# A one-core transformer block: output tiles inside a batch's last attention unit, next tokens prepared a unit earlier, denominators ahead of values

## What is computed

```python
def _tc_rmsnorm(x, t, gw, gb, bw, bb):
    g = (t @ gw.T + gb)[:, None, :]
    b = (t @ bw.T + bb)[:, None, :]
    inv_rms = jax.lax.rsqrt(jnp.mean(x * x, axis=-1, keepdims=True) + EPS)
    return g * x * inv_rms + b

def _attention(x, Wq, Wk, Wv, Wo):          # 16 heads of 32
    q, k, v = ((x @ W.T).reshape(B, L, H, dh) for W in (Wq, Wk, Wv))
    attn = jnp.einsum('blhd,bmhd->bhlm', q, k) / scale
    p = jax.nn.softmax(attn, axis=-1)
    o = jnp.einsum('bhlm,bmhd->blhd', p, v).reshape(B, L, D)
    return o @ Wo.T

x1 = x + _attention(_tc_rmsnorm(x, t, g1w, g1b, b1w, b1b), Wq, Wk, Wv, Wo)
y = x1 + _swiglu(_tc_rmsnorm(x1, t, g2w, g2b, b2w, b2b), gate_w, hid_w, out_w)
out = x + y
```

## Time and profile before

| | |
|---|---|
| median of 3 runs | 2479.52 us (2472.38 to 2492.58) |
| the profiled execution | 2483.76 us, of which the span 2481.9 us |
| busy: PE | 2309.7 us (93%) |
| busy: PE weight loads | 1572.9 us (63%) |
| busy: DVE | 1676.2 us (68%) |
| busy: ACT | 1310.9 us (53%) |
| busy: POOL | 1454.4 us (59%) |
| mean granted TensorE clock | 0.976 of full speed |

### The profile page before, as it was taken

How to read it: one execution, slowest core, us unless ns; L and a number is a source line. 1 busy time by engine, 2 the same in 40 slices (tenths; PEclk the granted TensorE clock), 3 DMA queues, 4 the chain that set the end, 5 groups by cost and what they waited for, 6 DMA issues and landing times. The chain is left out here.

```text
span 2481.9 us, 40287 instructions
## 1 busy us (share of the span) xinstructions
PE 2309.7 (93%) x10884; PEld 1572.9 (63%) x10884; DVE 1676.2 (68%) x2732; ACT 1310.9 (53%) x2319; POOL 1454.4 (59%) x1351
## 2 busy tenths in 40 slices
PE   5999989999989999989999848999999999999999
PEld 4655436554447555456554336888888888888887
DVE  4776734667725776537777347887788778778877
ACT  3366762566752667734667724445444534454454
POOL 0388981689970888944889925731572166216711
PEclk8999999999989999999999978999999999999999
DMA  5212203212122122132222043115412541254125
GB/s 179 81 41 63 64 14 108 52 41 67 48 71 64 38 69 52 47 95 52 51 57 60 21 162 136 60 60 179 151 54 69 170 154 52 74 164 157 47 81 174
DMA packets 92656, 209.60 MB, mean 84 GB/s; under 512 B 15632, under 2 KB 15632, under 8 KB 90640
## 3 DMA queue, kind: packets, MB, share of 16 engines
q1 hardware_dynamic: 91344, 202.71, 27.2%
q0 software_dynamic: 1088, 4.19, 0.4%
HBM read 134.23 MB, written 19.92 MB: 62 GB/s over the span
## 5 line engine op out<-in xcount | busy, mean ns | idle before, releaser
L680 DVE TENSOR_REDUCE pmax<-bank 128x1 f32<-128x512 f32 x1024 | 653.7, 684 | 197.0 <-PE bank L893 187.6
L599 ACT ACTIVATE probs<-bank 128x512 f32<-128x512 f32 x1024 | 572.0, 600 | 330.6 <-PE bank L973 249.5
L447 POOL TENSOR_TENSOR sums<-sums,probs 128x512 f32<-128x512 f32 x512 | 641.4, 1291 | 0.5 <-ACT probs L599 0.5
L447 POOL TENSOR_TENSOR sums<-probs 128x512 f32<-128x512 f32 x256 | 320.4, 1282 | 380.6 <-ACT probs L599 258.9
L973 PE MATMUL bank<-qs,ks 128*128 128x512 f32 x1024 | 441.3, 439 | 40.0 <-ACT probs L599 37.9
L893 PE MATMUL bank<-ks,qs 96*128 96x512 f32 x1024 | 402.9, 406 | 25.8 <-DVE pmax L680 25.1
L973 PEld LDWEIGHTS bank<-qs,ks 128*128 128x128 f32 x1024 | 192.8, 191 | 323.4 <-ACT probs L599 167.3
L1536 PE MATMUL bank<-H_hi,wt_hi 128*128 128x512 f32 x896 | 350.0, 391 | 14.6 <-DVE H_lo L1391 14.6
L1550 PE MATMUL bank<-ow,aw 128*128 128x512 f32 x1536 | 358.7, 392 | 0.0
L1536 PE MATMUL bank<-H_lo,wt_hi 128*128 128x512 f32 x896 | 349.6, 390 | 0.0
L1536 PE MATMUL bank<-H_hi,wt_lo 128*128 128x512 f32 x896 | 349.5, 390 | 0.0
(11 more groups left out here) (139 smaller groups left out, 3233.8 us busy)
## 6 DMA issues: line engine op xcount, KB each, us to landing
raw<-in_gu_w SPq DMA_DIRECT2D x66, 512.0 KB, 3.6
wo_raw<-in_out_w SPq DMA_DIRECT2D x128, 256.0 KB, 2.6
ks<-qk_hi SPq DMA_DIRECT2D x136, 128.0 KB, 2.4
qs<-qk_hi SPq DMA_DIRECT2D x264, 64.0 KB, 2.0
x<-in_x SPq DMA_DIRECT2D x10, 1024.0 KB, 5.2
ks<-qk_lo SPq DMA_DIRECT2D x68, 128.0 KB, 2.4
qs<-qk_lo SPq DMA_DIRECT2D x132, 64.0 KB, 2.0
wv<-wv_parts SPq DMA_DIRECT2D x4, 2048.0 KB, 8.9
```

Source lines behind the costliest of these rows:

```text
L447: nc.gpsimd.tensor_tensor(sums[:, h, :], first, probs[:, s % 2, h, :], ALU.add) \
L599: nc.scalar.activation(probs[:, s % 2, h, :], sbank[i % SB][:], ACT.Exp, scale=SCALE).then_inc(st_done, 1)
L680: nc.vector.reduce_max(pmax[:, t, h, hf:hf + 1], mbank[n % MB][:], AX_X).then_inc(sq_done, 1)
```

## The change

- **Steps.** hT moves from units 5 and 7 to (unit, step) (4,15), (4,18), (4,24), (5,8) and (6,14), (6,17), (6,24), (7,0). What goes ahead of it moves too: `load_x` of the first half from SP's turn in unit 3 to unit 1, squares from (4,4) to (3,4) and from (6,3) to (5,5), the inverse roots on POOL from (4,5) to (3,6) and from (6,6) to (6,0), the scaling from (4,6) to (4,1) and from (6,7) to (6,2). The squares' unused output goes to a slot of `qk_hi` instead of `yout`. Projections of Q stand at every step, not every second one; the last K tile moves from step 26 of unit 7 to step 13.
- **Output tiles 0 and 1** stand in unit 7, two products a step, from steps 18 and 24. Their operand is split at (3,3) and (4,1), that of tile 2 at (7,1), and for these three ACT first copies the tokens to a free PSUM bank (`mspare`), from which both halves of the split are made.
- **Order.** Where a key tile has both, `denominators` stands ahead of `values`.
- **Sums.** Head 0 of quad 0 adds into a slot of `yout`, not `sums`, and POOL waits for the D product at its second add of a quad, not at the first.
- **Last key tile of a batch.** POOL doesn't add it (4 adds); TensorE multiplies `probs` by the ones directly (4 more products in that D product).
- **Normalising** the last two units' `o` moves from POOL to DVE; for unit 6 through a copy of `den` in `mspare` that ACT makes.
- **Tail.** D product, then tiles 2 to 7. SP waits for the D product before it loads `wv`.

```diff
@@ -32,17 +32,20 @@
 IN_V = {1: ("Q", 1), NT - 3: ("K", 2, 0), NT - 2: ("mT", 0)}
 UNIT = NS * GH
-PROJECTED = {("K", 2, 1): (0, 1), ("Q", 2): (9, 2)}
+PROJECTED = {("K", 2, 1): (0, 1), ("Q", 2): (9, 1)}
 for odd in (1, 3):
     PROJECTED.update({("Q", odd + 2): (odd * UNIT, 1), ("K", odd + 3, 0): (odd * UNIT + 14, 1),
-                      ("K", odd + 3, 1): ((odd + 1) * UNIT, 1), ("Q", odd + 3): ((odd + 1) * UNIT + 9, 2)})
-PROJECTED.update({("Q", NU - 1): (5 * UNIT, 1), ("Q", NU): (6 * UNIT + 8, 2), ("K", NU, 0): (7 * UNIT + 8, 1),
-                  ("K", NU, 1): (7 * UNIT + 26, 1)})
-HT_AT = {5: (9, 13, 17, 24), 7: (13, 16, 19, 23)}
+                      ("K", odd + 3, 1): ((odd + 1) * UNIT, 1), ("Q", odd + 3): ((odd + 1) * UNIT + 9, 1)})
+PROJECTED.update({("Q", NU - 1): (5 * UNIT, 1), ("Q", NU): (6 * UNIT + 8, 1), ("K", NU, 0): (7 * UNIT + 8, 1),
+                  ("K", NU, 1): (7 * UNIT + 13, 1)})
+HT_AT = {(4, 15): (0, 0), (4, 18): (1, 0), (4, 24): (2, 0), (5, 8): (3, 0),
+         (6, 14): (0, 1), (6, 17): (1, 1), (6, 24): (2, 1), (7, 0): (3, 1)}
 SUMS_AT = {(5, 1): (0, 0), (1, 1): (1, 1)}
 MAXIMA_AT = (6, 3)
+EARLY_OUT = {18: 0, 24: 1}
+SPLIT_AT = {(3, 3): 0, (4, 1): 1, (7, 1): 2}
 VALUES_AT = (3, 1, 3, 2)
 SB, MB = 3, 3
...
                         stack(b, ("Q", u + 2), (u + 2) % 3)
-                    if u == 3:
+                    if u == 1:
                         load_x(b, 0, prepared)
...
-                hold(sp, held, sum_done, sums_done(b, NU - 1, NS - 1, GH - 1))
+                hold(sp, held, w_ready, MISC(b, misc_index(True, ("D", NU - 1, 1)) + 1))
                 load_wv()
...
-                        if (u, s) == (4, 5):
+                        if (u, s) == (3, 6):
                             inverse_root(b, b * 2 + 2)
-                        if (u, s) == (6, 6):
+                        if (u, s) == (6, 0):
                             inverse_root(b, b * 2 + 3)
-                        if s == 4 and u:
+                        if s == 4 and 0 < u < NU - 1:
                             normalise(b, u - 1)
+                        if n == NU * NS - 1:
+                            pool.wait_ge(sum_done, sums_done(b, u, s - 1, GH - 1))
+                            pool.sem_inc(sum_done, GH)
+                            break
                         for h in range(GH if s % QT else 0):
                             pool.wait_ge(st_done, SCORES_T(b, NT + n * GH + h + 1) + SB)
-                            if s % QT == 1 and h == 0:
+                            if (u, s, h) == (0, 1, 0):
+                                pool.wait_ge(y_stored[0], b * (NT // 2 * 16) + 16)
+                            if s % QT == 1 and h == 1:
                                 pool.wait_ge(w_ready, MISC(b, sums_before(u, s // QT)))
                             if s % QT > 1:
                                 pool.wait_ge(sum_done, sums_done(b, u, s - 1, h))
-                            first = probs[:, 0, h, :] if s % QT == 1 else sums[:, h, :]
-                            nc.gpsimd.tensor_tensor(sums[:, h, :], first, probs[:, s % 2, h, :], ALU.add) \
+                            total = sum_place(s // QT, h)
+                            first = probs[:, 0, h, :] if s % QT == 1 else total
+                            nc.gpsimd.tensor_tensor(total, first, probs[:, s % 2, h, :], ALU.add) \
...
                     act.wait_ge(sq_ready, SCORES_Q(b, NU * NMAX + t - 1))
-                nc.scalar.activation(osplit[:, t % 2, 0, :, :], o[:, :, t * P:(t + 1) * P],
-                                     ACT.Copy).then_inc(os_act, 1)
+                tokens = o[:, :, t * P:(t + 1) * P]
+                if t in SPLIT_AT.values():
+                    up = mspare[:].rearrange("p (g c) -> p g c", g=NG)
+                    if t:
+                        act.wait_ge(os_dve, b * NT + t)
+                    nc.scalar.activation(up, tokens, ACT.Copy).then_inc(o_up, 1)
+                    act.wait_ge(o_up, b * len(SPLIT_AT) + (t + 1))
+                    tokens = up
+                nc.scalar.activation(osplit[:, t % 2, 0, :, :], tokens, ACT.Copy).then_inc(os_act, 1)
+            def denominators_up(b):
+                act.wait_ge(den_ready, b * (NU - 1) + (NU - 1))
+                act.wait_ge(sq_done, SCORES_Q(b, (NU - 1) * NMAX + NMAX) + MB)
+                nc.scalar.activation(mspare[:], den[:], ACT.Copy).then_inc(den_up, 1)
             def weight_hi(w):
...
-                            if (u, s) == (4, 4):
+                            if (u, s) == (3, 4):
                                 square(b, 0, h)
-                            if (u, s) == (4, 6):
...
                                 output(b, u - 1)
-                        if u == NU - 1 and s >= NS - 2:
-                            output_hi(b, s - (NS - 2))
+                            if u == NU - 1 and (s, h) == (2, 3):
+                                denominators_up(b)
+                            if u == NU - 1 and (s, h) in SPLIT_AT:
+                                output_hi(b, SPLIT_AT[s, h])
                 output(b, NU - 1)
-                for t in range(2, NT):
+                for t in range(len(SPLIT_AT), NT):
...
                     link(nc.vector.reciprocal(pair[:, 1, :], cols[:, :, 0]))
+                elif part == 2 and u == NU - 1:
+                    link(nc.vector.transpose(den[:], pair[:, 1, :].unsqueeze(2).to_broadcast([P, QB // 32, 32])))
+                elif part == 2:
+                    nc.vector.transpose(den[:], pair[:, 1, :].unsqueeze(2).to_broadcast([P, QB // 32, 32])).then_inc(den_ready, 1)
                 else:
-                    nc.vector.transpose(den[:], pair[:, 1, :].unsqueeze(2).to_broadcast([P, QB // 32, 32])).then_inc(den_ready, 1)
+                    dve.wait_ge(od_act, b * NU + (u + 2))
+                    if u < NU - 1:
+                        dve.wait_ge(den_up, b + 1)
+                    cols = o[:, u // 2, u % 2 * QB:(u % 2 + 1) * QB]
+                    nc.vector.tensor_tensor(cols, cols, den[:] if u == NU - 1 else mspare[:], ALU.mult).then_inc(on_done, 1)
...
+                def lo_part(t):
+                    dve.wait_ge(os_act, b * NT + t + 1)
+                    tokens = o[:, :, t * P:(t + 1) * P]
+                    if t in SPLIT_AT.values():
+                        tokens = mspare[:].rearrange("p (g c) -> p g c", g=NG)
+                    nc.vector.tensor_tensor(osplit[:, t % 2, 1, :, :], tokens,
+                                            osplit[:, t % 2, 0, :, :].bitcast(F32), ALU.subtract).then_inc(os_dve, 1)
...
                                     work_tile(b, tile)
-                            if s == 3 and u and h < 3:
+                            if s == 3 and 0 < u < NU - 1 and h < 3:
                                 normalise(b, u - 1, h)
-                def lo_part(t):
-                    dve.wait_ge(os_act, b * NT + t + 1)
-                    nc.vector.tensor_tensor(osplit[:, t % 2, 1, :, :], o[:, :, t * P:(t + 1) * P],
-                                            osplit[:, t % 2, 0, :, :].bitcast(F32), ALU.subtract).then_inc(os_dve, 1)
+                            if s == 2 and u == NU - 1 and h < 3:
+                                normalise(b, u - 1, h)
+                            if (u, s, h) == (NU - 1, 3, 0):
+                                normalise(b, u - 1, 3)
+                            if u == NU - 1 and (s, h) in SPLIT_AT:
+                                lo_part(SPLIT_AT[s, h])
                 def out_tile(t):
                     n = NU * NMAX + t
...
-                for t in range(2):
-                    lo_part(t)
                 out_tile(0)
-                for t in range(2, 4):
-                    lo_part(t)
+                lo_part(len(SPLIT_AT))
                 work_tile(b, ("D", NU - 1, 1))
-                for part in range(3):
+                for part in range(4):
                     normalise(b, NU - 1, part)
                 for t in range(1, NT):
...
-                pe.wait_ge(sum_done, sums_done(b, u, QT * quad + QT - 1, GH - 1))
+                direct = (u, quad) == (NU - 1, QUADS - 1)
+                pe.wait_ge(sum_done, sums_done(b, u, QT * quad + QT - 1 - direct, GH - 1))
                 for h in range(GH):
-                    last = nc.tensor.matmul(wbank[DH * h:DH * h + DH, :], ones[:], sums[:, h, :], start=True, stop=True)
+                    last = nc.tensor.matmul(wbank[DH * h:DH * h + DH, :], ones[:], sum_place(quad, h), start=True,
+                                            stop=not direct)
+                for h in range(GH if direct else 0):
+                    last = nc.tensor.matmul(wbank[DH * h:DH * h + DH, :], ones[:], probs[:, (NS - 1) % 2, h, :], start=False,
+                                            stop=True)
                 last.then_inc(w_ready, 1)
+            def out_tile(b, t, steps):
+                steps = [(k, a, c) for k in range(NG) for a, c in ((0, 0), (0, 1), (1, 0))][steps]
```

(26 more changed lines are left out.)

44 lines of the change are left out of this document (29 added, 15 removed).

## The result

The changed kernel takes **2466.69 us** (median of 15 runs, 2462.11 to 2472.02); beside it the kernel before took 2479.52 (15 runs, 2472.38 to 2492.58). The ratio is 0.9949, 95% interval 0.9938 to 0.9961: 13 us gained, not the 60 forecast, and the time lies outside the range. The profiled execution took 2466.27 us (span 2464.4, mean clock 0.975).

A forecast was written before the change was run, and what follows sets the result against it. TensorE, nearly full, was taken as the bound, POOL as second limit. Gains of 15.0 us a batch, 60 for four, plus 2.5 took the profiled 2483.8 to 2421.3; it said 2420, range 2400 to 2446.

The forecast's parts named there:

- is POOL's chain and hardly anything else: Unit 5 before, 31.83 us, taken as bounded by POOL's 31.3; 0.5 us a batch to be gained.
- last tail, beyond these: Batch 3's tail: stores and next loads start earlier, gaining 2.5 us more than the other tails' 5.0.
- D product first, POOL's wait later: Units 0, 1, 2, 5: POOL's first add runs beside the D product; gains 0.4, 1.2, 1.2, 0.5 us.
- Projections at every step only fill a step that was empty.: Attention's projections, at every step instead of every second: claimed to fill empty steps, with no cost charged.
- Unit 6: Earlier scaling, and inverse root inside the D product wait, leave about 33.2 us; gain 3.0, bounds 1 and 4.
- Unit 7: Fewer turns, two output tiles added, no last POOL adds: 31.7 us against 35.5, gain 3.8, bounds 2 and 5.
- the early tiles wait: Rival, unit 7: tile 0 or 1 stops TensorE 3 us each, 24 in all, 2444 us; chance 0.08.
- the clock stays low: Rival, unit 7: two units at clock 0.86 keep their 3.6 us over batch 3's, 2428 us; chance 0.05.
- Tail: Two output tiles leave, four products enter: 21 us against 26.4, gain 5.0; one store wait, 2 us taken.
- held by transfers: Rival, tail: store waits take 2 us from each of three tails, 7.5 from the last; 2433 us, chance 0.12.
- TensorE is full already: Rival: units 0 to 5 give nothing back; only unit 6, unit 7 and tail gain, 2436 us; chance 0.18.
- The D product blocks: Rival: 60 D products ahead of value products wait for POOL; at 2 us a place, 2537 us; chance 0.03.

The follow-up runs named there:

- the census: The kernel before with eight extra 128x4 tensor_scalar instructions a batch on DVE, in units 1, 2, 3 and 5: 2482.24 us, ratio 1.0004.

## Why the prediction was wrong

**The step that failed.** The prediction prices the loads, the squares, the inverse root and the turns, and has no term for the mean of squares, which moves with them from (4,5) to (3,5) and from (6,5) to (5,7) on DVE. It was put at nothing without being named. It cost 37.4 us: unit 5 came out 7.2 us longer where the prediction had it 0.5 shorter, and unit 3 gave back 0.2 us where it gives 1.9 without that instruction. The view that would have shown the danger was at hand: the group of this instruction in the kernel before has a mean of 1457 ns, for four numbers a partition. It takes nine times its own time there, each time to 0.03 us behind the end of a POOL instruction; so POOL's work beside it decides how long it lasts, and the change moved it to where the last eight of a row of adds were still to end. The prediction used the Trainium skill, SBUF — State Buffer, Who interferes with whom, only for the rest parts with two SBUF inputs, and gave its rule without its condition: an instruction with at most one SBUF input stays out of the contention only outside the modes that use both port pairs. The same section also names tensor_scalar among the VectorE instructions that can enter a mode which takes the port shared with GpSimd, and says that tensor_reduce never does on trn2. The runs agree with both: tensor_scalar 0.16 to 8.84 us, tensor_reduce 0.14 to 0.16 us at the same places. That it is this port is the section's account; the runs show who waits for whom, not the port.

That unit 5 "is POOL's chain and hardly anything else" was right, and was the reason: that chain, close-packed, is what the instruction waits out.

**By terms**, us a batch, mean of the batches. "Cleared" is the fourth experiment, which is the changed kernel without the held mean and with the two Q projections spread again.

| stretch | predicted | after | cleared |
|---|---|---|---|
| V product and unit 0 | -0.4 | +0.6 | -0.4 |
| unit 1 | -1.2 | -1.9 | -2.0 |
| unit 2 | -1.2 | +0.6 | -1.2 |
| unit 3 | -0.3 | -0.2 | -1.9 |
| unit 4 | +0.4 | +0.3 | +0.7 |
| unit 5 | -0.5 | +7.2 | -1.1 |
| unit 6 | -3.0 | -2.1 | -1.3 |
| unit 7 | -3.8 | -5.2 | -5.0 |
| tail | -5.0 | -3.1 | -4.2 |
| last tail, beyond these | -2.5 | -1.4 | +0.9 |

The last row is the last tail alone (35.92 before, 31.38 after, 32.61 cleared) less the other tails' gain.

- *D product first, POOL's wait later.* Under-sized: 1.9 and not 1.2 in unit 1, which went to 32.98 while TensorE was thought to need 33.4. The 33.41 busy us of before were no floor: the same 173 recorded matmuls take 32.87 after. In unit 2 the 1.2 came only with the projections spread. Each edit was undone with the other in place: the order is then worth 1.6 us in all (not told from nothing), the later wait 9.7.
- *"Projections at every step only fill a step that was empty."* Wrong: 11.2 us in all. Unit 2 has TensorE full, and products set close together empty the steps that had them before. In unit 2 of batch 1 TensorE waits three times for DVE's maxima, 0.2 to 0.5 us each and 0.9 in all, and once, 0.3, with the projections spread; that is 0.6 of the unit's 1.0 us. What makes up the rest of the 11.2 us is not shown.
- *Unit 6.* The gain came, over-sized: 2.1 us of 3.0 (1.3 cleared). TensorE's work was about right (32.16 us busy, 32.8 taken), but it waits 2 us more, 1.57 of them at one place, for a rest part of the turned tokens on DVE (L699), where the prediction gave a turn up to 0.9.
- *Unit 7.* 30.27 us in batch 1, 30.36 in the mean, not 31.7, at a clock of 1.00 in place of 0.86: the early tiles stop next to nothing (0.6 us ahead of 16 `wo_hi` products), and the rival "the early tiles wait" falls, as does "the clock stays low". TensorE's sum of 31.1 was too high, it is busy 28.92. The copies into the bank did what they were for: the 12 rest parts that read a bank take 0.69 us each, beside POOL's adds too, where two a batch took 1.0 to 1.2 before.
- *Tail.* The chain over DVE ended as worked out. The store took 9.0 us from its issue at 724.4, TensorE's wait was 2.9 (2 taken, bounds 0 to 3.3), and behind it the products ran at 0.47 to 0.63 us until 738.8; the tail's granted clock is 0.93. Issuing the store earlier and ahead of `wv` gave 15.1 us over four tails, 3.8 each: the place that the rival "held by transfers" named, where it had 2.
- *"TensorE is full already"* falls: with the held mean gone, units 1 and 3 gave 1.9 to 2.0 us each. *"The D product blocks"* falls too: TensorE's longest wait for POOL ahead of a D product in batch 1 is 0.2 us after, and 0.9 cleared, at the start of unit 6 (0.5 before), where the rival had 2 us at every place.

With the held mean gone and the projections spread, the kernel takes 2418.05 us, 2 us from the forecast. That closeness is luck: it needs two edits that the change does not have, and terms are off by 1 to 2 us in both directions and cancel, a batch by 16.4 us and not 15.0, the last tail by 3.4 the other way. As a forecast of this change it was wrong.

## What to carry to other kernels

List every instruction that a step takes along when it is moved, the smallest too, and look up in the trace of before how long each takes against its own size: if one lasts many times its due, find out what it waits for, since its price at the new place is what that neighbour does there, here 8.8 us for 0.16. In this kernel a small tensor_scalar on DVE with both sides in SBUF did not belong among close-packed POOL instructions with something waiting behind it; as a reduction it took 0.15 us there. And in a queue shared by a small urgent store and a large load, the order is worth trying both ways: here one store, issued early and ahead of 2 MB, was 15 us.

## What was not expected of the hardware

The Trainium skill, SBUF — State Buffer, Who interferes with whom, says that whichever engine issues first has the shared pair for its whole instruction while the other is blocked. The trace goes further: in unit 5 the DVE instruction was held through seven ends of POOL instructions in a row, in every batch, by 8.8 us. In the census it got in at the first end 24 times of 32. It is not its operand (a constant is held just as long) and not readiness of POOL's next instruction alone: at the seven ends of unit 5 the next add's exponential had ended 1.1 to 3.1 us before, and at ends where the census's were let in 1.4 to 3.0 us before. What decides at which end it is let in stays open; the trace shows that it differs by place and mostly repeats from batch to batch (at (2,7) three batches of four). The other side of it was not seen: POOL's adds beside a held instruction take 1.25 to 1.31 us, and all adds of the changed kernel 1.26 to 1.31.
